# A graph layer on one core: the low halves of the x2 tiles are subtracted by GpSimd instead of VectorE

## The reference, cut to what matters

```python
xn = _layernorm(x)
x = x + _gnn(xn, W, a, src, dst) + _mix(xn[None], wq, wk, wv, wo, ln1_g, ln1_b, ...)[0]
x = x + _ffn(_layernorm(x)[None], w_gate, w_up, w_down)[0]

# _gnn: e = exp(-leaky_relu(al[src] + ar[dst]));  segment sums of e and of e * h[dst] over src
# _mix: x2 = _layer_norm(x, ln1_g, ln1_b);  q, k, v = x2 @ wq + bq, x2 @ wk + bk, x2 @ wv + bv;  ...
```

## Time and profile before

| | us |
|---|---|
| median of 3 runs | 1284.93 (1282.96 to 1285.98) |
| profiled execution, its own time | 1283.55 |
| span of the profiled execution | 1281.8 |
| PE busy / PEld busy in the span | 1196.6 / 1050.0 |
| DVE busy / ACT busy / POOL busy | 756.2 / 705.5 / 338.4 |
| mean granted clock of PE | 0.967 of full speed |
| front: first matmul of the next stage | 156.00 |

### The profile page before, as it was taken

How to read it: one execution, slowest core, us unless ns; L and a number is a source line. 1 busy time by engine, 2 the same in 40 slices (tenths; PEclk the granted TensorE clock), 3 DMA queues, 4 the chain that set the end, 5 groups by cost and what they waited for, 6 DMA issues and landing times. The chain is left out here.

```text
span 1281.8 us, 19485 instructions
## 1 busy us (share of the span) xinstructions
PE 1196.6 (93%) x6857; PEld 1050.0 (82%) x6857; DVE 756.2 (59%) x1244; ACT 705.5 (55%) x1069; POOL 338.4 (26%) x296
## 2 busy tenths in 40 slices
PE   6989889999999999999559998899999998999997
PEld 4555689999999999999547876899988786887884
DVE  7988815656565666656543664777755122556646
ACT  8275628777777777777755432322245432355544
POOL 1500004242332324242111110266653332111100
PEclk9999999999999999999759999899998999999999
DMA  8001220022020202021145452522244332711103
GB/s 215 10 20 29 46 77 1 18 53 69 0 69 0 69 0 69 4 65 64 55 150 168 159 167 95 186 84 85 84 118 158 97 96 60 221 44 47 34 19 97
DMA packets 72194, 99.41 MB, mean 78 GB/s; under 512 B 27241, under 2 KB 52165, under 8 KB 71631
## 3 DMA queue, kind: packets, MB, share of 16 engines
q1 hardware_dynamic: 68684, 86.11, 23.1%
q0 software_dynamic: 3456, 12.58, 3.2%
HBM read 77.04 MB, written 21.63 MB: 77 GB/s over the span
## 5 line engine op out<-in xcount | busy, mean ns | idle before, releaser
L1146 POOL TENSOR_TENSOR cos_sin_lo<-cos_sin,cos_sin_hi 125x1024 fp32r<-125x1024 f32 (+1 forms) x40 | 95.4, 2384 | 248.6 <-ACT cos_sin_hi L1234 248.6
L468 PE MATMUL p_cnt<-hot_s,hot_d 125*125 125x418 bf16 x540 | 112.7, 359 | 1.8 <-DVE hot_d L401 1.8
L705 PE MATMUL p_h<-x 128*125 128x512 f32 x400 | 110.3, 403 | 0.0
L399 DVE TENSOR_SCALAR hot_s<-iota_h,ends 125x1250 bf16<-125x1250 f16 x180 | 97.6, 542 | 14.4 <-PE p_cnt L468 12.3
L1468 PE MATMUL p_w<-x,mix_hi_v 128*128 128x416 f32 (+1 forms) x384 | 105.2, 355 | 0.0
L468 PEld LDWEIGHTS p_cnt<-hot_s,hot_d 125*125 125x125 bf16 x540 | 62.4, 138 | 51.5 <-DVE hot_d L401 41.4
L1468 PE MATMUL p_w<-x,mix_hi_q 128*128 128x416 f32 (+1 forms) x384 | 104.2, 352 | 0.0
L1468 PE MATMUL p_w<-x,mix_hi_k 128*128 128x416 f32 (+1 forms) x384 | 104.1, 352 | 0.0
L966 PE MATMUL rows_in_psum<-h_hi,a_lo 125*125 125x342 f32 x300 | 96.7, 322 | 2.7 <-DVE a_lo L910 2.7
L966 PE MATMUL rows_in_psum<-h_lo,a_hi 125*125 125x342 f32 x300 | 96.7, 322 | 0.0
L966 PE MATMUL rows_in_psum<-h_hi,a_hi 125*125 125x342 f32 x300 | 96.7, 322 | 0.0
(11 more groups left out here) (297 smaller groups left out, 3055.6 us busy)
## 6 DMA issues: line engine op xcount, KB each, us to landing
x_in<-in_x_dram SPq DMA_DIRECT2D x30, 448.0 KB
attn_dram<-attn_t SPq DMA_DIRECT2D x8, 625.0 KB, 3.9
at_in<-attn_dram SPq DMA_DIRECT2D x10, 500.0 KB, 4.6
x_rows<-in_x_dram SPq DMA_DIRECT2D x10, 448.0 KB
x_in<-gnn_dram SPq DMA_DIRECT2D x10, 448.0 KB
out_dram<-rows SPq DMA_DIRECT2D x10, 448.0 KB
mix_in_v<-in_L_mix_wv_dram SPq DMA_DIRECT2D x8, 512.0 KB, 6.0
mix_in_k<-in_L_mix_wk_dram SPq DMA_DIRECT2D x8, 512.0 KB, 4.7
```

Source lines behind the costliest of these rows:

```text
L399: dve.tensor_scalar(hot_s[:, j, :], iota_h[:], ends[:, at, 0:1].rearrange("p a b -> p (a b)"), None, ALU.is_equal)
L468: last = pe.matmul(p_cnt[0:T, t % 2, n, 0:w], hot_d[:, j, 0:T], hot_s[:, j, a:a + w], start=False, stop=False)
L705: last = pe.matmul(p_h[0:T, i % 2, n, :], left[i % 2][:, k, :], right[:, k, cols], start=(k == 0 and m == 0), stop=(k == K8 - 1 and m == 2))
L1146: pool.tensor_tensor(full(cs_lo, k), full(cs, k), f32(full(cs_hi, k)), ALU.subtract).then_inc(s_cslo[0], 1)
```

## The change

The ten subtractions leave DVE's program. They are appended to POOL's, behind the inverse roots, in the order 0 to 9, each with its wait for `s_hi`. The operands, the shape and the semaphore `s_lo` are the same. DVE's tiles of one-hots now follow one another with nothing between them.

```diff
@@ gpsimd @@
             pool.tensor_tensor(core.ln_shift[:], core.xn_shift[:], core.rstd2[:], ALU.mult).then_inc(s_rstd, 1)
+            for i in range(NT):
+                pool.wait_ge(s_hi, i + 1)
+                cols = slice(i * T, (i + 1) * T)
+                pool.tensor_tensor(x2_lo[:, :, cols], x2[:, i % 2], f32(x2_hi[:, :, cols]), ALU.subtract).then_inc(s_lo, 1)
@@ vector @@
-            def keep_lo(i):
-                dve.wait_ge(s_hi, i + 1)
-                cols = slice(i * T, (i + 1) * T)
-                dve.tensor_tensor(x2_lo[:, :, cols], x2[:, i % 2], f32(x2_hi[:, :, cols]), ALU.subtract).then_inc(s_lo, 1)
@@
                 tile_onehots(1)
                 for t in range(2, NT):
-                    for i in AFTER[t - 2]:
-                        keep_lo(i)
                     tile_onehots(t)
-                for i in AFTER[NT - 2]:
-                    keep_lo(i)
                 dve.wait_ge(core.mix_hi_ready[VALUE], 1)
```

## The result

The changed kernel takes 1300.2 us (median of 4 runs, 1298.66 to 1303.52) where the kernel before takes 1285.45 (4 runs). The ratio is 1.0115, 95% interval 1.0089 to 1.0142: 14.8 us more, 11.4 to 18.3 by the interval. Forecast were 1298.3 and 13.4 more.

The account below looks back on a forecast made before the run. DVE was taken to set the pace inside chunk loops, PE between tiles. Stalls less relief +11.0 and clock falls +2.4 gave 13.4 us on 1284.93, so 1298.3 us, range 1291 to 1304.

Parts of the forecast that it names:

- Pace and cover: Counting tiles: DVE sets the pace inside chunk loops, PE between tiles; removing 11.9 us of DVE work gains only 0.60.
- The lock: Chunk loops: a POOL subtraction of 2.355 us shuts DVE's one-hots out of SBUF, a stall of 2.03 us each.
- low half 1: Ahead of tile 4, all slots full: POOL ends at 86.58, DVE wanted to go on at 85.04; cost 1.40 us.
- Which instruction is caught: Inside a chunk: POOL lets `hot_s` pass, slips in under `hot_d`, and the next `hot_s` waits, 2.03 us.
- sign of being wrong: New trace: `hot_s` staying at 0.54 us beside a POOL operation would mean sharing; about 2.6 us was expected.
- Low half 8: Under tile 8's last one-hots: tile 9 closes about 0.4 us later, but ACT hides it; cost 0.
- The clock: TensorE after long stalls in chunk loops: two of five bring a clock fall at 1.2 us each, +2.4 us.
- The sum: Front, all low halves: 1.40 + 2.03 + 2.03 - 0.60 + 6.09 = 10.95, +11.0 us before clock falls.
- the five stalls: Low halves 2, 4, 5, 6 and 7 fall mid-loop and cost 2.03 us each.
- Half sharing: Rival: ports shared, not locked, for `hot_s`; at half the stalls +5.2 us, 1290.1; chance 0.09 including no stall.
- Relief: Rival: DVE's 1.11 us between tiles is on the path at nine places, 10.0 us less, 1274.9; chance 0.03.
- a fall of the clock at every stall: Rival, chunk loops: five falls at 1.7 us are 8.5, together 19.5 us more, 1304.4 or more; chance 0.05.

Follow-up runs that it names:

- e4_covered: Kernel before with only low halves 0, 3 and 9 moved to POOL, the other seven on DVE: ratio 0.9999, the front 71.3 us, -0.5.
- e6_gate: Changed kernel, but POOL holds low halves 1 to 8 until the pause between two tiles: ratio 1.0050 against the kernel before, +6.4 us.
- e1_nosub: Changed kernel with the subtractions left out, a 125x1 POOL operation keeping each wait and signal: ratio 1.0014 against the kernel before, the front 71.3 us.
- e2_half: Changed kernel with POOL doing features 0 to 499 of each low half, DVE the others between tiles: ratio 1.0058 against the kernel before, +7.4 us.
- e5_only8: Kernel before with only low half 8 moved to POOL, the other nine on DVE: ratio 1.0015, +1.9 us; the front 73.8 us.
- the first profile: Profiled execution of the changed kernel, no further edit: span 1299.4 us against 1281.8 for the kernel before.
- the second: Changed kernel profiled again on another occasion, no edit: 1299.24 us, ratio 1.0110 against the kernel before; profiled span 1295.9 us.

## Why the prediction was right

- *Pace and cover.* Right. DVE sets the pace in the loops, so a hold-up there passes whole to the tile (tiles 6 and 7: +1.89 each; `hot_d` 2.15 instead of 0.26). Where DVE waits for slots anyway it is hidden (e4_covered), between two tiles about two thirds of it (e6_gate). The moved 11.9 us brought 0.5 back, forecast 0.60.
- *The lock.* Right in kind. Taking away the length takes away the cost (e1_nosub), halving it halves it (e2_half). The forecast took 2.355 us for the POOL operation from the earlier trace rows; it took 2.12 (the same shape at another place, and why it is shorter is not shown), and so a hold-up is 1.89 and not 2.03. At low half 1 it is 1.70 - 0.54 = 1.16, forecast 1.40. The rule cited from the Trainium skill, "SBUF — State Buffer", "Who interferes with whom", agrees with these rows: a one-hot under a long POOL operation waits for its end. Which property of the one-hots brings them into it no run here shows, since all runs have the same one-hots.
- *Which instruction is caught.* Wrong. I had POOL slipping in under `hot_d` and `hot_s` waiting. In mid-loop it is `hot_d` that waits, every time; `hot_s` is caught only where DVE had been idle (85.39, 1.70 us). The earlier trace rows could not tell the two apart: the 125x10 operation really works for 0.20 us, less than the 0.23 that a meeting hides, so a waiting `hot_d` would look like a free one. In mid-loop it makes no difference, one chunk is late either way. By its letter the prediction's own sign of being wrong, `hot_s` at 0.54 beside a POOL operation, came true; it stood for shared ports, and the 2.15 us of `hot_d` shows that it was a badly chosen sign.
- *Low half 8.* Here it does. The step "under the last one-hots of tile 8 ... 0" failed: with `hot_d` caught, tile 8's last chunk is late and the cost is 1.87 (e5_only8).
- *The clock.* The count of two new falls is met by the first profile, but that is luck: the second has one. The price of 1.2 us a fall was too small, it is 1.5 to 1.6.
- *The sum.* Without new falls it would be 11.3, put together from the undisturbed tiles of both profiles (no run shows such a front); forecast 11.0. That this is so near is luck in part: the five stalls and low half 1 came out 0.9 smaller, low half 8 1.87 larger, and the rest, -0.6, lies in tiles 3 and 4, probably because the fall between them lies elsewhere than before. With two falls it is 14.4 (forecast 13.4), and the whole time rose by 14.8.
- *The rivals.* Half sharing is refuted by the lengths: a hold-up is POOL's whole 2.12 us less 0.23, and POOL's operation does not grow beyond its wait. e2_half alone would not do it, since a shared port would cost half for half the length too. Relief is refuted by e1_nosub (0.5 us), a fall of the clock at every stall by both profiles (two of six, one of six).

## What to carry to other kernels

Idle time of POOL is not free room while DVE works on SBUF with such operations: before giving POOL an elementwise operation, look which DVE instruction will stand beside it and whether DVE has slack there. Put it where DVE waits for someone else (low half 3), and price it in a loop whose pace DVE sets at nearly POOL's whole length, with the pause that TensorE gets and the clock that it may lose. And a busy-time account (12 us off a busy engine, onto an idle one) had the wrong sign here; a timeline of both engines had the right one, and 13.4 of the 14.8 us, in part by errors that cancelled.

## What had not been expected of the hardware

A `tensor_scalar` of only 125 elements waits for POOL (0.26 to 2.15 us) as one of 1250 does (0.54 to 2.42 in e6_gate). A POOL fill that reads nothing holds it up too (0.94 us, 0.67 lost). And a stretch in which TensorE stood still for 1.8 us in one piece was followed by a fall of its clock in two of six hold-ups in one execution and in one of six in another, at different tiles, with nothing else changed: the same tile 5 took 12.54 us in one and 10.96 in the other. What decides it is not shown.
